# A two-layer graph attention kernel: head 0's denominators and reciprocals moved into its attention product, and its sources' row made by one small product and a VectorE transpose

## The chip, the cores and the metric

The kernel runs on one core of a Trainium2 chip. The metric is the device time of one execution in microseconds. Before the change the median of three runs is 637.04 us (636.98 to 637.24). About 0.2% (1.27 us) is what such a measurement tells from no change.

## The reference

x has 512 nodes of 768 features; the graph has 16896 edges (self loops among them). Two graph attention layers are computed, the first with 8 heads of 768, the second with one, then a residual and a layer norm:

```python
def gat_layer(x, W, a_s, a_d, b, edge_index, concat):
    h = (x @ W).reshape(n, H, C)
    alpha_s = jnp.einsum('nhc,hc->nh', h, a_s)
    alpha_d = jnp.einsum('nhc,hc->nh', h, a_d)
    e = jax.nn.leaky_relu(alpha_s[src] + alpha_d[dst], NEG_SLOPE)
    m = jax.ops.segment_max(e, dst, num_segments=n)
    e = jnp.exp(e - m[dst])
    denom = jax.ops.segment_sum(e, dst, num_segments=n)
    alpha = e / (denom[dst] + EPS)
    msg = h[src] * alpha[:, :, None]
    out = jax.ops.segment_sum(msg, dst, num_segments=n)
    return out + b
...
h = jax.nn.elu(gat_layer(x, W1, ...))
x = _layernorm(x + gat_layer(h, W2, ...))
```

## The kernel before

The edges become a dense 512x512 matrix of counts CT (how often node s is a source of node d), built by products of one-hot blocks on TensorE, 132 blocks of 128 edges. A mask Mk is 0 where there is an edge and very negative elsewhere. With these, each head is dense work in tiles of 128 nodes (NT = 4) and 128 features (FT = 6):

- stage B: h = x W1 of the head, in 8 half products of 18 matmuls (`half_B`); high and low parts of x and W1 give three products each. ScalarE copies each half product from PSUM to h32 (`evict_B`). VectorE takes two sums over each row of h (`sums_h`): asd, the source and the target term of each node.
- the row of sources: the 512 source terms must lie along the free dimension, the same on all partitions, in the PSUM bank "as" of the head. `sources` makes it. For heads 0, 1 and 7 TensorE transposes a broadcast column, four times (`broadcast`, L1303). For heads 2 to 6 VectorE spreads the column over 16 columns (`source_columns`, L803), TensorE sums it with a 128x128 pattern in one product of 16 moving columns (L1311), and VectorE turns the result with a 128x512 transpose (`source_row`, L810).
- scores: VectorE's `maxima` reads that row and the mask (L837, four operations), `terms` makes small columns from the maxima (L844, L846 and three more), `columns` and `rows` turn them into rows, and `scores` on ScalarE and VectorE gives L = exp(...) times CT, and Ph and Pl, its high and low parts.
- denominators: for head 0, y2, the sum of L over the source tiles, goes through four products with two columns of ones (`denominators`, L1339; each fp32 product is two passes, so the profile shows eight). VectorE adds EPS and takes the reciprocal of a 128x4 tile dcl (L907, L909), TensorE turns it into rows by four transposes (`reciprocals`, L1347), and ScalarE copies them to rb (L495). Other heads have another way to rb.
- stage A: the attention product, one per 128 features: 12 matmuls of 512 columns (`stage_A`, L1357, L1360, L1363). VectorE scales it by rb (`scale_A`, L916), then `elu` (L922, L924) and `low_g` (L928), with ScalarE's exp (L510) and high part (L517) between.
- stage C: the head's share of layer 2, added up in the six O banks.

Each engine's program is written out by hand, in the order in which it runs, with semaphore waits between engines. An engine that waits holds up all that stands behind it in its own program. The PSUM banks are O0 to O5 and R0, R1. Uses of R alternate in the order of a list RING, and `take` waits until the use two places back was read. Uses listed in OWN have a fixed O bank and no such wait.

Around the change TensorE's program is: edge blocks, head 1's half products 4 to 7 (with the transposes of CT's mask ahead of number 6, L1432, and then head 0's sources; in the last one also `columns(0)`, L1322), head 2's half products 0 to 3, denominators of head 0, stage A of head 0 for c = 0 to 5 (reciprocals after the second tile of c = 0; sources of head 1 ahead of c = 1), head 2's half products 4 to 7, then stage C of head 0. The last four take the R banks in turn: number 6 waits until ScalarE has copied number 4, number 7 until it has copied number 5. ScalarE's program has these two copies (L455) within its work on head 0's activation:

```python
if h == 0:
    reciprocals()
    e.wait_ge(s_asd, 18)
    high_w2(0, 0)
    high_w2(0, 1)
for c in range(FT):
    exp_y(h, c)
    if c:
        high_g(h, c - 1)
    if h == 0 and c < 2:
        high_w2(0, c + 2)
    if h == 0 and c == 4:
        evict_B(2, 2, 0)
high_g(h, FT - 1)
if h == 0:
    evict_B(2, 2, 1)
```

`high_w2` (L443) gives the high part of a tile of W2; GpSimd's `low_w2` (L1195) waits for it and gives the low part. VectorE's program after head 0's scores is: two low parts of P (L894), L907 and L909, row sums of head 2's first tile (L768), `maxima` (L818, L837) and `terms` of head 1, two more row sums, then `scale_A` and the rest for c = 0 to 5.

Of the kernel before, what the change touches and what calls it, by code (L numbers as in the profile page):

```python
# [5 lines left out]
def gat_resnorm_kernel(nc, x, xT, src, dst, W1, as1, ad1, b1c, W2, as2, ad2, b2, out):  # L6
# [64 lines left out]
    with ctx:  # L71
# [97 lines left out]
        def abc_slot(h):  # L169
# [6 lines left out]
        R = [ctx.enter_context(nc.psum_tensor(f"R{i}", [128, 512], f32)) for i in range(2)]  # L176


        OWN = {("B", 0, 2): O[4], ("B", 0, 3): O[5], ("as", 0, 0): O[4], ("as", 1, 0): O[5], ("den", 0, 0): O[4],
               ("x", 0, 0): O[0], ("r1", 0, 0): O[1], ("x", 1, 0): O[2], ("r1", 1, 0): O[3],  # L180
               ("A", 0, 0): O[2], ("A", 0, 1): O[3], ("A", 0, 2): O[0], ("A", 0, 3): O[1], ("A", 0, 4): O[4], ("A", 0, 5): O[5]}

# [71 lines left out]
        def released(use):  # L254

            kind, h, n = use
            if kind == "B":
                return s_h32, 8 * h + n + 1
            if kind == "al":
                return s_ar, 1  # L260
            if kind == "at":
                return s_asd, 8 * H + 1
            if kind == "as":
                return s_amx, NT * h + NT
            if kind == "xs":
                return s_srow, h - 1
            if kind == "x":
                return s_row, 2 * h + 2
            if kind == "r1":
                return s_lk, NT * (h + n) + NT  # L270
            if kind == "den":
                return (s_dc, h) if 0 < h < EARLY else (s_rc, h + 1)
            if kind == "A":
                return s_y, FT * h + n + 1
            return s_dn0, h + 1
# [443 lines left out]
        def vector_program(e):  # L719
# [79 lines left out]

            def source_columns(h):  # L800

                e.wait_ge(s_asd, 8 * h + 8)
                e.tensor_tensor(asm[:, :, :], by_quarter(asd[:, h % 2, 0, :]), by_tile, ALU.mult).then_inc(s_asm, 1)  # L803

            def source_row(h):
                cols = ring_bank("xs", h, 0)[:, 0:NT * 4]
                e.wait_ge(s_bc, bc_value(h, 0))

                e.wait_ge(*released(RING[RING_AT["as", h, 0] - 2]))
                e.transpose(ring_bank("as", h, 0)[:, :].rearrange("p (c j) -> p c j", j=32), cols.unsqueeze(2).broadcast_to([128, NT * 4, 32])).then_inc(s_srow, 1)  # L810

            def maxima(h, lo, hi, bank):


                if h == 0:
                    e.wait_ge(s_four, 11)
                e.wait_ge(s_asd, 8 * h + 8 if h < H else 8 * H + 1)
                e.tensor_tensor(adm[:, :, :], by_quarter(asd[:, h % 2, 1, :]), by_tile, ALU.mult).then_inc(s_adm, 1)  # L818
                if 2 <= h < H - 1:
                    source_row(h)  # L820
                for t in range(lo, hi):
                    if t == 0:
                        if 2 <= h < H - 1:
                            e.wait_ge(s_srow, h - 1)
                        else:
                            e.wait_ge(s_bc, bc_value(h, 0))
                        if h >= EARLY:
                            e.wait_ge(s_A, FT * h)
                    if h == 0:
                        e.wait_ge(s_mk, t + 1)  # L830
                    if 0 < h < EARLY:

                        if t:
                            e.wait_ge(s_amx, NT * h + t)
                        else:
                            e.wait_ge(s_asd, (18, 24)[h - 1])
                    e.tensor_tensor_reduce(  # L837
                        out=junk[:, 0:N] if 0 < h < EARLY else Pl[:, t, :], in0=bank[:, :], in1=Mk[:, t, :], op0=ALU.add, op1=ALU.max, scale=1.0, scalar=-3e38,
                        accum_out=amx[:, t:t + 1]).then_inc(s_amx, 1)
# [120 lines left out]
            for j in range(EJ):  # L960
                if FIRST <= j < FIRST + FT:
                    low_x(j - FIRST)
                    low_w1(0, j - FIRST)
                if j in (24, 30, 46, 70):
                    t = (24, 30, 46, 70).index(j)
                    if t == 0:
                        wait_abc(0)
                        e.wait_ge(s_xl, FT)
                    e.wait_ge(s_h32, 2 * t + 2)
                    sums_h(0, t, h32[:, t % 2, :], abc[:, 0, :, :])  # L970
                    low_h(0, t)
                if j in range(36, 36 + 6 * FT, 6):
                    low_w1(1, (j - 36) // 6)
                if j in range(78, 78 + 6 * 4, 6):
                    low_w1(2, (j - 78) // 6)
                if j in (44, 76, 98, 124):
                    accumulate((44, 76, 98, 124).index(j))
                one_hot(j)
            wait_abc(1)
            e.wait_ge(s_h32, 10)  # L980
            sums_h(1, 0, h32[:, 0, :], abc[:, 1, :, :])
# [280 lines left out]
        def tensor_program(e):  # L1262
# [42 lines left out]

            def sources(h, ready):

                if 2 <= h < H - 1:
                    bank = take("xs", h, 0)
                    e.wait_ge(s_asm, h - 1)  # L1310
                    e.matmul(bank[:, 0:NT * 4], four[:, :], asm[:, :, :].rearrange("p t b -> p (t b)"), start=True, stop=True).then_inc(s_bc, 1)  # L1311
                    return
                bank = take("as", h, 0)
                e.wait_ge(s_asd, ready)
                broadcast(bank, asd[:, h % 2, 0, :], range(NT))
# [24 lines left out]
                                 start=d == 0, stop=True, skip_group_check=True)  # L1340
                m.then_inc(s_den, 1)

            def reciprocals():

                e.wait_ge(s_rc, 1)
                for d in range(NT):
                    m = e.transpose(ring_bank("den", 0, 0)[:, 128 * d:128 * d + 128], dcl[:, d:d + 1].broadcast_to([128, 128]), idn[:, :])  # L1347
                m.then_inc(s_rt, 1)

            def stage_A(h, c):  # L1350
                bank = take("A", h, c)
                for t in range(NT):
# [8 lines left out]
                    if c == 0:  # L1361
                        e.wait_ge(s_hl, NT * h + t + 1)
                    m = e.matmul(bank[:, :], hl[:, t, cs], Ph[:, t, :], start=False, stop=t == NT - 1)  # L1363
                    if h == 0 and c == 0 and t == 1:
                        reciprocals()
                m.then_inc(s_A, 1)

            def stage_C(h, c, groups=range(6), between=None, ends=True, at=2):
# [54 lines left out]
                count_block(j)  # L1423

            for n in range(4, 8):
                if n == 6:
                    e.wait_ge(s_cst, 4)
                    e.wait_ge(s_ji, 2 * len(GROUPS))
                    e.wait_ge(s_ms, NT)
                    for d in range(NT):  # L1430
                        for s in range(NT):
                            m = e.matmul(O[d][:, 128 * s:128 * s + 128], ohd[:, s, 128 * d:128 * d + 128], idb[:, :],  # L1432
                                         start=s == 0, stop=True, skip_group_check=True)
                        m.then_inc(s_mt, 1)
                    sources(0, 8)
                half_B(1, n // 2, n % 2, take("B", 1, n),
                       (lambda: columns(0, ring_bank("x", 0, 0))) if n == 7 else None)
            for n in range(4):
                half_B(2, n // 2, n % 2, take("B", 2, n))
            denominators(0)  # L1440
            for c in range(FT):
                if c == 1:
                    sources(1, 16)
# [156 lines left out]
```

## Time and profile before

| what | value |
|---|---|
| median of 3 runs | 637.04 us |
| the profiled execution | 636.94 us, span 635.0 us |
| TensorE matmuls busy | 626.7 us (99%) |
| TensorE weight loads busy | 536.9 us (85%) |
| VectorE busy | 536.8 us (85%) |
| ScalarE busy | 337.6 us (53%) |
| GpSimd busy | 210.6 us (33%) |
| mean granted TensorE clock | 0.998 |
| chain that ended last | TensorE 85%, VectorE 10% |

Times in the profile count from the span's start. PE is TensorE's matmuls, PEld its weight loads, DVE VectorE, ACT ScalarE, POOL GpSimd. In a timeline the columns are start, time taken, engine, line, operation, output and inputs, count, and in brackets the idle time before it and who ended it. Starts are given as issued; an operation that is held up inside its engine shows as a long one. Successive matmuls overlap, so a matmul's own time is longer than the distance to the next. In the chain of waits the pieces stand end to end, and each piece's time is what it adds.

### The profile page before, as it was taken

What the parts mean: (1) busy time and instruction counts of PE and PEld (TensorE: products, weight loads), DVE (VectorE), ACT (ScalarE), POOL (GpSimd) and SP (SyncE); (2) the same over time, 40 slices, a digit from 0 to 9 for tenths busy, and PEclk for the clock granted to TensorE, in tenths of its full rate; (3) what the DMA queues carried; (4) which work ended last, traced back from release to release, by engine and by line L of the source; (5) the groups of instructions that cost most, each with busy time, mean ns of one, the idle gap of its engine ahead of it and who ended that gap; (6) DMA issues with size and microseconds to landing.
All of it is one profiled execution on the core that took longest, in us unless ns stands there. A gap on an engine that the chain in (4) does not pass through costs nothing.

```text
span 635.0 us, 9251 instructions
## 1 busy us (share of the span) xinstructions
PE 626.7 (99%) x3353; PEld 536.9 (85%) x3362; DVE 536.8 (85%) x974; ACT 337.6 (53%) x570; POOL 210.6 (33%) x133
## 2 busy tenths in 40 slices
PE   9999999999999999999999999999999999999996
PEld 5766568989888898989899988999898989887885
DVE  8999997989989887778686958797798869898967
ACT  7899992545625645553354635363445344534282
POOL 2000000131643834076405840384208540451230
PEclk9999999999999999999999999999999999999999
DMA  8422403116153423043302520260217130500002
GB/s 321 161 71 81 148 27 100 50 51 199 34 166 122 153 98 102 1 141 109 100 0 71 179 65 11 76 224 19 81 40 233 52 100 6 218 26 0 1 2 99
DMA packets 22172, 59.34 MB, mean 93 GB/s; under 512 B 2544, under 2 KB 2800, under 8 KB 22128
## 3 DMA queue, kind: packets, MB, share of 16 engines
q1 hardware_dynamic: 21984, 58.69, 28.0%
q8 instruction: 27, 0.44, 0.3%
q14 instruction: 17, 0.14, 0.1%
q10 hardware_dynamic: 144, 0.07, 0.0%
HBM read 54.03 MB, written 4.72 MB: 93 GB/s over the span
## 4 chain that ended last, share of the span: by engine, by line
PE 85%; DVE 10%; issue 1%; ACT 1%; DMA 1%; POOL 1%; ACTq 0%; DVEq 0%
PE O L1390 27%; PE R L1281 8%; PE R L1287 8%; PE R L1284 8%; PE O L1298 7%; PE R L1357 6%; PE R L1363 6%; PE R L1360 6%; DVE ohd L728 1%; DVE L L885 1%; PE O L1357 1%; PE O L1363 1%; PE O L1360 1%; PE O L1539 1%; PE O L1545 1%
## 5 line engine op out<-in xcount | busy, mean ns | idle before, releaser
L1195 POOL TENSOR_TENSOR W2l<-Wr,W2h 128x768 fp32r<-128x768 f32 x48 | 91.9, 1935 | 133.3 <-ACT W2h L443 133.3
L1281 PE MATMUL R<-W1h,xTh 128*128 128x384 f32 x312 | 106.1, 340 | 0.4 <-ACT h L455 0.4
L1199 POOL TENSOR_TENSOR Pl<-L,Ph 128x512 fp32r<-128x512 f32 x34 | 55.9, 1662 | 152.4 <-ACT Ph L491 152.4
L1287 PE MATMUL R<-W1h,xTl 128*128 128x384 f32 x312 | 104.8, 336 | 0.0
L1284 PE MATMUL R<-W1l,xTh 128*128 128x384 f32 x312 | 104.8, 336 | 0.0
L1189 POOL TENSOR_TENSOR W1l<-Wr,W1h 128x768 fp32r<-128x768 f32 x30 | 59.6, 2010 | 116.9 <-ACT W1h L432 116.8
L768 DVE CUSTOM_DVE_ANT_0 junk<-h,abc 128x768 bf16<-128x768 f32 x64 | 66.9, 1046 | 23.2 <-ACT h L455 21.6
L1390 PE MATMUL O<-W2h,gh 128*128 128x256 f32 (+1 forms) x384 | 78.2, 338 | 0.0
L1390 PE MATMUL O<-W2h,gl 128*128 128x256 f32 (+1 forms) x384 | 77.8, 337 | 0.0
L1390 PE MATMUL O<-W2l,gh 128*128 128x256 f32 (+1 forms) x384 | 77.2, 335 | 0.0
L1357 PE MATMUL R<-Ph,hh 128*128 128x512 f32 x168 | 66.3, 395 | 0.0
L1363 PE MATMUL R<-Ph,hl 128*128 128x512 f32 x168 | 65.9, 392 | 0.0
L1390 PEld LDWEIGHTS O<-W2l,gh 128*128 128x128 f32 x384 | 59.0, 188 | 7.9
L1360 PE MATMUL R<-Pl,hh 128*128 128x512 f32 x168 | 65.3, 389 | 0.0
L1390 PEld LDWEIGHTS O<-W2h,gl 128*128 128x128 f32 x384 | 58.7, 188 | 7.7
L1390 PEld LDWEIGHTS O<-W2h,gh 128*128 128x128 f32 x384 | 58.3, 188 | 6.5 <-issue 0.2
L1281 PEld LDWEIGHTS R<-W1h,xTh 128*128 128x128 f32 x312 | 58.5, 188 | 2.4 <-ACT h L455 1.2
L443 ACT CAST W2h<-Wr 128x768 fp32r<-128x768 f32 x48 | 37.9, 832 | 42.0 <-DVE rm L853 19.2
L1298 PE MATMUL O<-ohd,ohs 128*128 128x512 bf16 x255 | 59.1, 379 | 1.1 <-DVE ohs L732 0.4
L455 ACT COPY h<-R 128x384 f32<-128x384 f32 x62 | 29.4, 475 | 57.1 <-PE R L1287 54.6
L1284 PEld LDWEIGHTS R<-W1l,xTh 128*128 128x128 f32 x312 | 58.5, 188 | 0.6
L1287 PEld LDWEIGHTS R<-W1h,xTl 128*128 128x128 f32 x312 | 58.5, 188 | 0.0
(201 smaller groups left out, 1178.3 us busy)
## 6 DMA issues: line engine op xcount, KB each, us to landing
Wr<-in_W SPq DMA_DIRECT2D x101, 384.0 KB, 3.6
abc<-in_as SPq DMA_DIRECT2D x9, 384.0 KB, 4.1
abc<-in_ad SPq DMA_DIRECT2D x9, 384.0 KB, 5.3
h_rows<-h SPq DMA_DIRECT2D x8, 384.0 KB, 2.3
hl<-h_rows SPq DMA_DIRECT2D x8, 384.0 KB, 5.9
xin<-in_xT SPq DMA_DIRECT2D x6, 256.0 KB, 5.7
xr<-in_x SPq DMA_DIRECT2D x1, 1536.0 KB, 7.7
out<-res SPq DMA_DIRECT2D x4, 384.0 KB, 2.3
```

Of the source, the lines that this page charges most:

```text
L768: e.tensor_tensor_reduce(out=junk[:, :], in0=get, in1=a_ap[:, i, :], op0=ALU.mult, op1=ALU.add, scale=1.0, scalar=0.0, accum_out=asd[:, h ...
L1189: e.tensor_tensor(W1l[:, k, :], Wr[:, n, :], W1h[:, k, :].bitcast(f32), ALU.subtract).then_inc(s_w1l, 1)
L1195: e.tensor_tensor(W2l[:, m % N2, :], Wr[:, n, :], W2h[:, m % N2, :].bitcast(f32), ALU.subtract).then_inc(s_w2l, 1)
L1199: e.tensor_tensor(Pl[:, t, d0:d1], L[:, t, d0:d1], Ph[:, t, d0:d1].bitcast(f32), ALU.subtract).then_inc(s_Pl, 1)
L1281: e.matmul(bank[:, 0:HALF], xTh[:, f, xs], hi[:, ws], start=f == 0, stop=False)
L1284: e.matmul(bank[:, 0:HALF], xTh[:, f, xs], lo[:, ws], start=False, stop=False)
L1287: m = e.matmul(bank[:, 0:HALF], xTl[:, f, xs], hi[:, ws], start=False, stop=f == FT - 1)
L1298: e.matmul(O[2 * (g % 2) + q][:, :], ohs[:, r, 128 * q:128 * q + 128], ohd[:, r, :], start=j == STARTS[g], stop=j == STARTS[g + 1] - 1).th ...
L1357: e.matmul(bank[:, :], hh[:, t, cs], Ph[:, t, :], start=t == 0, stop=False)
L1360: e.matmul(bank[:, :], hh[:, t, cs], Pl[:, t, :], start=False, stop=False)
L1363: m = e.matmul(bank[:, :], hl[:, t, cs], Ph[:, t, :], start=False, stop=t == NT - 1)
L1390: mm = e.matmul(ob, ga[:, c, 128 * t:128 * t + 128], wa[:, q, lo:hi], start=first and (hi - lo == 512 or t % 2 == 0), stop=last, skip_grou ...
```

## The change

Two things are done, both for head 0 alone.

Head 0's row of sources is made in the way of heads 2 to 6: `source_columns(0)` stands on VectorE behind the last edge block, one product of 16 columns into O5 ahead of head 1's half product 5, and VectorE's transpose from O5 to O4 after the first step of `maxima(0)`.

`denominators(0)` no longer stands ahead of stage A but in its first product (c = 0), after the second tile, where the reciprocals were; the reciprocals go to the same place in the second product (c = 1).

```diff
-        OWN = {("B", 0, 2): O[4], ...
+        OWN = {("xs", 0, 0): O[5], ("B", 0, 2): O[4], ...
...
             if kind == "xs":
-                return s_srow, h - 1
+                return s_srow, h
...
             def source_columns(h):
+                if h == 0:
+                    e.wait_ge(s_four, 11)
...
             def source_row(h):
                 cols = ring_bank("xs", h, 0)[:, 0:NT * 4]
                 e.wait_ge(s_bc, bc_value(h, 0))
-                e.wait_ge(*released(RING[RING_AT["as", h, 0] - 2]))
+                if h:
+                    e.wait_ge(*released(RING[RING_AT["as", h, 0] - 2]))
...
-                if 2 <= h < H - 1:
+                if h != 1 and h < H - 1:
                     source_row(h)
                 for t in range(lo, hi):
                     if t == 0:
-                        if 2 <= h < H - 1:
-                            e.wait_ge(s_srow, h - 1)
+                        if h != 1 and h < H - 1:
+                            e.wait_ge(s_srow, max(h, 1))
...
                 one_hot(j)
+            source_columns(0)
             wait_abc(1)
...
             def sources(h, ready):
-                if 2 <= h < H - 1:
+                if h != 1 and h < H - 1:
                     bank = take("xs", h, 0)
-                    e.wait_ge(s_asm, h - 1)
+                    e.wait_ge(s_asm, max(h, 1))
...
-            def reciprocals():
+            def reciprocals_0(h):
...
-                    if h == 0 and c == 0 and t == 1:
-                        reciprocals()
+                    if h == 0 and c < 2 and t == 1:
+                        (denominators, reciprocals_0)[c](0)
...
             for n in range(4, 8):
+                if n == 5:
+                    e.wait_ge(s_four, 6)
+                    sources(0, 8)
                 if n == 6:
...
-                    sources(0, 8)
...
-            denominators(0)
             for c in range(FT):
```

The order of instructions moves as follows; the changed kernel's line numbers are 3 to 7 higher than the old ones behind the first edit. On TensorE, from the last matmul of head 2's half product 3 into stage A of head 0 (oner holds ones, dcl the reciprocals, idn the identity), before:

```order
L1287 MATMUL R<-W1h,xTl 128x384
L1339 MATMUL O<-oner,y 128x2 x4
L1357 MATMUL O<-Ph,hh 128x512
L1360 MATMUL O<-Pl,hh 128x512
L1363 MATMUL O<-Ph,hl 128x512
L1357 MATMUL O<-Ph,hh 128x512
L1360 MATMUL O<-Pl,hh 128x512
L1363 MATMUL O<-Ph,hl 128x512
L1347 MATMUL O<-idn,dcl 128x128 x4
L1357 MATMUL O<-Ph,hh 128x512
```

and after the change, from the third matmul of the first product's first tile:

```order
L1367 MATMUL O<-Ph,hl 128x512
L1361 MATMUL O<-Ph,hh 128x512
L1364 MATMUL O<-Pl,hh 128x512
L1367 MATMUL O<-Ph,hl 128x512
L1343 MATMUL O<-oner,y 128x2 x4
L1361 MATMUL O<-Ph,hh 128x512
L1364 MATMUL O<-Pl,hh 128x512
L1367 MATMUL O<-Ph,hl 128x512
L1361 MATMUL O<-Ph,hh 128x512
L1364 MATMUL O<-Pl,hh 128x512
L1367 MATMUL O<-Ph,hl 128x512
L1307 MATMUL O<-idn,asd 128x128 x4
```

The denominators stand six attention matmuls later than before. The reciprocals no longer stand in this product; head 1's source transposes (L1307) come ahead of them, and then six matmuls of the second product, behind which they stand.

On VectorE, at the start of head 0's maxima, before:

```order
L768 ISA asd 128x1
L818 TENSOR_TENSOR adm<-asd,quad 128x16
L837 ISA Pl,amx<-O4,Mk 128x512
L837 ISA amx 128x1
L837 ISA Pl,amx<-O4,Mk 128x512
```

and after:

```order
L768 ISA asd 128x1
L821 TENSOR_TENSOR adm<-asd,quad 128x16
L813 STREAM_TRANSPOSE O4<-O5 128x512
L840 ISA Pl,amx<-O4,Mk 128x512
L840 ISA amx 128x1
```

The transpose is new there. All else on VectorE, but for the small multiply behind the last edge block, keeps its order, and so do ScalarE, GpSimd and SP.

## Rows read from the trace of the kernel before

**Rows 1.** Waits of TensorE's weight loads, 145:635: who, for whom, us, times, longest.
```profile
PEld R L1281 <- ACT h L455: 1.2, 3, 0.7
```
**Rows 2.** Timeline of ScalarE's copies of h, then of TensorE's weight load.
```profile
151.58 0.47 ACT L455 COPY h<-R 128x384 f32<-128x384 f32 x1
...
155.21 0.47 ACT L455 COPY h<-R 128x384 f32<-128x384 f32 x1
...
155.73 0.19 PEld L1281 LDWEIGHTS R<-W1h,xTh 128*128 128x128 f32 x1 [0.24 <-ACT h L455]
```
**Rows 3.** Chain that ended last, 107:114: start, us added, engine, tile, line, count.
```profile
108.06 0.44 PE O L1303 x4
...
113.05 0.17 PE R L1287
113.22 0.14 PE O L1322 x2
113.36 0.26 PE R L1281
```
**Rows 4.** The same chain at head 0's denominators, and at the tail's (L1553).
```profile
127.64 1.02 PE O L1339 x8
128.67 0.34 PE O L1357
129.01 0.23 PE O L1360
...
619.33 0.79 PE R L1553 x8
```
**Rows 5.** Timeline of TensorE: head 2's fourth half product's end, and the reciprocals.
```profile
127.16 0.34 PE L1287 MATMUL R<-W1h,xTl 128*128 128x384 f32 x1
...
130.00 0.60 PE L1347 MATMUL O<-idn,dcl 128*128 128x128 f32 x4
```
**Rows 6.** The line of heads 2 to 6's transpose: ns min/median/max.
```profile
L810 DVE STREAM_TRANSPOSE R<-R x5: 721/731/732, 180.6 to 475.2; 128x512 f32<-128x512 f32 x5
```
**Rows 7.** Timeline of VectorE, 108:139.
```profile
108.53 0.69 DVE L837 CUSTOM_DVE_ANT_0 Pl<-O,Mk 128x512 fp32r<-128x512 f32 x1 [1.30 <-PE O L1303]
...
115.57 0.96 DVE L768 CUSTOM_DVE_ANT_0 junk<-h,abc 128x768 bf16<-128x768 f32 x1 [0.47 <-ACT h L455]
...
128.71 0.16 DVE L907 TENSOR_SCALAR dcl<-O 128x4 f32<-128x4 f32 x1
...
131.00 0.17 DVE L818 TENSOR_TENSOR adm<-asd,quad 128x16 f32<-128x16 f32 x1
132.47 0.69 DVE L837 CUSTOM_DVE_ANT_0 junk<-O,Mk 128x512 bf16<-128x512 f32 x1 [1.30 <-PE O L1303]
...
135.40 0.30 DVE L844 TENSOR_TENSOR zm<-amx,asd 128x4 f32<-128x4 f32 x1
135.74 0.18 DVE L846 TENSOR_TENSOR zmm<-zm,quad 128x16 f32<-128x16 f32 x1
...
138.22 1.28 DVE L916 TENSOR_TENSOR L<-O,rb 128x512 f32<-128x512 f32 x2
```
**Rows 8.** Timeline of ScalarE's copy to rb, and of GpSimd's first pair.
```profile
130.64 0.59 ACT L495 COPY rb<-O 128x512 f32<-128x512 f32 x1 [2.62 <-PE O L1347]
...
132.03 3.65 POOL L1195 TENSOR_TENSOR W2l<-Wr,W2h 128x768 fp32r<-128x768 f32 x2 [5.81 <-ACT W2h L443]
```
**Rows 9.** Timeline at head 6's terms: GpSimd, then VectorE.
```profile
475.14 3.67 POOL L1189 TENSOR_TENSOR W1l<-Wr,W1h 128x768 fp32r<-128x768 f32 x2 [27.30 <-ACT W1h L432]
478.77 1.84 POOL L1195 TENSOR_TENSOR W2l<-Wr,W2h 128x768 fp32r<-128x768 f32 x1
...
478.50 0.33 DVE L844 TENSOR_TENSOR zm<-amx,asd 128x4 f32<-128x4 f32 x1
478.86 1.78 DVE L846 TENSOR_TENSOR zmm<-zm,quad 128x16 f32<-128x16 f32 x1
```
**Rows 10.** Stretch behind the last matmul: us, each engine's busy us, PEclk, DMA share, GB/s.
```profile
629.70:632.60 2.90, 0.00 (x0) 0.00 (x0) 2.09 (x6) 0.98 (x2) 0.00 (x0) 0.96 0.64 257
```

More of the change, by code:

```diff
@@ L176, in gat_resnorm_kernel @@
         R = [ctx.enter_context(nc.psum_tensor(f"R{i}", [128, 512], f32)) for i in range(2)]
-        OWN = {("B", 0, 2): O[4], ("B", 0, 3): O[5], ("as", 0, 0): O[4], ("as", 1, 0): O[5], ("den", 0, 0): O[4],
+        OWN = {("xs", 0, 0): O[5], ("B", 0, 2): O[4], ("B", 0, 3): O[5], ("as", 0, 0): O[4], ("as", 1, 0): O[5], ("den", 0, 0): O[4],
                ("x", 0, 0): O[0], ("r1", 0, 0): O[1], ("x", 1, 0): O[2], ("r1", 1, 0): O[3],
```

## The prediction

> **What bounds the kernel now.** I read the waits of TensorE's weight loads first, then TensorE's chain around the moved operations, then the timelines of VectorE, ScalarE and GpSimd from 107 to 156 us. Behind the edge counts TensorE sets the end, and waits only for fractions of a microsecond: for ScalarE's evictions of h it is 1.2 us in three places [rows 1], and one of the three, 0.24 us at 155.73, lies right behind this change [rows 2]. That place decides the forecast. Head 2's seventh and eighth half products share the two R banks with the fifth and sixth. ScalarE empties those only between its steps of head 0's activation (151.58 and 155.21, [rows 2]), and these follow VectorE's scale, ELU and low parts one for one. So between VectorE's first scaled tile of head 0 and the eviction at 155.21 **VectorE's chain and TensorE are level**, TensorE even 0.24 us early. Work saved on TensorE ahead of that place is worth nothing unless VectorE comes earlier too, and a delay of VectorE there is paid in full by the end.
>
> **TensorE, part by part.**
> 1. Head 0's sources. The four transposes take 0.44 us of the chain [rows 3]. The new product (16 moving columns) is nearest to the one with 32: 0.14 us, and 0.26 instead of 0.17 for the matmul behind it, 0.23 together [rows 3]. Gain 0.44 - 0.23 = 0.2 us (0.1 to 0.3, if the sides differ). It is issued one half product (18 matmuls of 0.17, 3.1 us) ahead of its old place, and its input comes from a VectorE step put right behind the last edge block, so nobody waits for it.
> 2. Head 0's denominators. They start only at 127.64, when VectorE's sum of the exponentials is there, while head 2's fourth half product ended at 127.16 + 0.34 = 127.50; the first attention matmul ends at 128.67 + 0.34 = 129.01 [rows 4, 5]. Without them it would end at 127.50 + 0.23 = 127.73, so they cost 1.28 us. Inside a running product the price is that of the same eight passes in the tail: 0.79 us, and 0.34 instead of 0.23 behind them, 0.90 together [rows 4]. Gain 0.38 us (between 0.1, if TensorE then meets VectorE's low part of block 1, and 0.5).
> 3. The reciprocals' four transposes are only moved: same count, same price.
>
> So TensorE would run 0.2 + 0.38 = 0.6 us earlier from 129 us on. That is all the change saves directly.
>
> **VectorE up to 127 us.** It gains a 16-column multiply and a 128x512 transpose, 0.73 us in five places now [rows 6], and loses the 1.30 us that it waits for TensorE's transposes before head 0's maxima [rows 7]. Later it waits 0.47 us for h at 115.57 anyway [rows 7], which levels the rest; from there it follows TensorE, 0.2 us earlier. I cost this part at nothing more; it would start to cost if the transpose ran over 1.0 us longer (0.57 + 0.47).
>
> **VectorE from 127 us.** The denominators now come behind six attention matmuls. The product starts at 127.16 + 0.17 - 0.2 = 127.1, six matmuls of 0.23 [rows 4] bring it to 128.5, and the passes take 1.02 us to their end [rows 4]: 129.5. VectorE's small step that stood at 128.71 is 0.8 us late. What lies behind it ran to 131.00 [rows 7], so VectorE is ready for head 1's maxima at 131.0 + 0.8 + 0.1 = 131.9. Now these start at 132.47, after 1.30 us of waiting for head 1's source transposes [rows 7]. Those start at 128.5 + 0.9 + 6 x 0.23 = 130.8 after the change and end 0.6 later, at 131.4: no longer in the way. Head 1's maxima, and its first term (135.40 now), come 0.6 us **earlier**: 134.8. Taken alone a gain.
>
> **What the move costs: GpSimd.** The reciprocals' transposes (130.00, [rows 5]) go behind head 1's source transposes and six matmuls of the second product: 130.8 + 0.44 + 6 x 0.23 = 132.6, that is 2.6 us later. ScalarE's copy to rb moves with them, from 130.64 to 133.25 [rows 8]. Behind that copy on ScalarE stand the first two high parts of W2, and GpSimd's low parts hang on them: two operations, 3.65 us, from 132.03 now [rows 8], from 134.65 to 138.3 then. Now they run beside head 1's maxima (132.47 to 135.4), which read one tensor in PSUM and one in SBUF and keep their 0.69 us [rows 7]. Then they will run beside head 1's terms and two row sums, which read two SBUF tensors each.
>
> What that does, the trace shows at head 6: GpSimd's pair ends at 478.81, its next operation at 480.61; VectorE's first term, issued at 478.50, takes 0.33 us and ends at 478.83; the second, issued at 478.86, takes 1.78 us and ends at 480.64 [rows 9]. A small two-tensor operation of VectorE is held until GpSimd's running one ends, and where GpSimd has another ready, that gets in and holds VectorE's next. Today's own row shows it in small: the term at 135.40 takes 0.30 us, to 135.70, and GpSimd's pair ends at 135.68 [rows 7, 8]. The Trainium skill ("Advanced Engine Details and Errata", GPSIMD Details) says that GpSimd shares a read and a write interface with VectorE and conflicts with its instructions that have two SBUF inputs. By that rule, which speaks against the change as these rows do, the sum has the same sign.
>
> Transferred: first term issued at 134.8, held by GpSimd's first operation (134.65 to 136.45); the second held by GpSimd's second, to 138.3. Now the second term ends at 135.74 + 0.18 = 135.92 [rows 7]. **VectorE is late by 138.3 - 135.9 = 2.4 us**, its first scaled tile comes at 140.6 instead of 138.22. From there to the eviction ScalarE's steps and GpSimd's next pair follow VectorE, and all of it moves as a whole: the evictions come at 154.0 and 157.6. TensorE, 0.6 us early, reaches head 2's seventh half product near 151.9, waits 2.5 us, waits 0.5 us more before the eighth, and starts that at 155.73 + 2.4 = 158.1.
>
> **Sum.** TensorE's 0.6 us end in that wait. What reaches the end is +2.4 us; what follows depends on TensorE and VectorE, both late by the same, so nothing takes it back. SP's two loads of W2 that wait for GpSimd's pair move by 2.6 us, tens of microseconds ahead of their use: nothing. The profiled execution took 636.94 us (span 635.0), 0.1 under the median of 637.04; so 639.3 for such a one, **639.4** for the median. Bounds: +1.9, if GpSimd's pair starts 0.5 us sooner than I have it, to +2.9, if it starts that much later: 638.9 to 640.0.
>
> **The rivals.**
> - *No hold (not slower).* VectorE's terms stay short. Then VectorE and TensorE are both 0.6 us early, and so is the end: 636.4. For it: GpSimd is only some 0.2 us ahead of the first term. Against: if it came behind, it would hold the second, and the sums behind are of the same kind. It decides if the pair starts over 2 us earlier, under the maxima as now.
> - *One hand-over.* GpSimd's first operation holds the term to 136.45, VectorE then keeps the way for the rest of the terms and the sums (2.8 us now, 135.40 to 138.22), and GpSimd's second waits. First scaled tile at 139.2, end +0.9: 637.9. Against: the second hand-over in [rows 9].
> - *TensorE's clock.* A TensorE gap of 2.5 us is new. Behind the last matmul of the kernel the granted clock over 629.70 to 632.60 is 0.96 [rows 10]: it fell to half (1.2 of 2.4 GHz) in the last 0.23 us of that stretch, after 2.7 us of idling. If it falls in the gap, the seventh half product takes 6.2 instead of 3.1 us and ends 1.2 us behind the eviction at 158.1: 640.6. The Trainium skill ("TensorE: Matmul & The Clock Gate", What's actually happening) says that the lower clock is the default and activity releases it; by it this case can occur, and the price is the same.
> - *Faster.* That would take 1.27 us and more; the whole saving is 0.6.
>
> **Chances and range.** My forecast 0.70; the clock's fall 0.07; one hand-over 0.06; no hold 0.14; faster by more 0.03. A measurement of this kernel can tell about 0.2% (1.27 us) from no change: faster 0.03, same 0.06 + 0.14 = 0.20, slower 0.77. The range takes in the forecast with its bounds, the one hand-over (637.9) and the clock (640.6): 637.8 to 640.8.
>
> **What would show it.** After: the denominators' passes at 0.9 us within the first product; ScalarE's copy to rb near 133.3; GpSimd's first pair near 134.7; head 1's first two terms at about 1.6 and 1.8 us; the first scaled tile near 140.6; TensorE's weight loads waiting for ScalarE's h before head 2's seventh and eighth half products, 3 us together. Wrong: terms of 0.15 us, GpSimd's pair under the maxima, or no TensorE wait between 150 and 160 us.

## The result, and the profile after

| | before | after |
|---|---|---|
| median of six executions | 637.13 us | 639.52 us |
| lowest to highest | 636.98 to 637.24 | 639.00 to 639.98 |
| profiled execution, its span | 636.94, 635.0 | 639.1, 637.3 |
| time after / before | | 1.0037 [1.0026, 1.0047] |

The change makes the kernel 2.4 us, 0.37%, slower. The six executions fall in two groups, 639.0 to 639.3 and 639.7 to 640.0 us; the one profiled is of the lower group. What parts the groups was found last (below).

The page of the changed kernel, its engine totals and the start of its chain by engine:

```profile
span 637.3 us, 9251 instructions
PE 627.4 (98%) x3351; PEld 537.1 (84%) x3360; DVE 540.7 (85%) x976; ACT 337.4 (53%) x570; POOL 210.6 (33%) x133
...
PE 75%; DVE 20%; issue 2%; ACT 1%; POOL 1%; DMA 1%; DVEq 0%; ACTq 0%
```

VectorE is busy 3.9 us longer than before and TensorE 0.7; the totals do not say where the end became 2.3 us later. The waits of TensorE's weight loads from 100 us on do (engine, line, what for: us in total, times, longest):

```profile
PEld R L1285 <- ACT h L455: 4.0, 4, 2.8
...
PEld O L1364 <- DVE Pl L897: 0.2, 1, 0.2
```

The first line stood at 1.2 us in three waits before [rows 1]; the second, a wait for VectorE's low part of P in the first attention product, is new and short. The timeline of the weight loads of the changed kernel around head 2's seventh and eighth half products:

```profile
151.87 0.19 PEld L1291 LDWEIGHTS R<-W1h,xTl 128*128 128x128 f32 x1
154.84 0.19 PEld L1285 LDWEIGHTS R<-W1h,xTh 128*128 128x128 f32 x1 [2.78 <-ACT h L455]
...
158.47 0.19 PEld L1285 LDWEIGHTS R<-W1h,xTh 128*128 128x128 f32 x1 [0.51 <-ACT h L455]
```

TensorE stands still for 2.78 us and then 0.51 us, and the eighth half product starts at 158.47 instead of 155.73 [rows 2]. To see why the evictions of h come late, follow VectorE and GpSimd 20 us earlier. VectorE of the changed kernel, from the denominators' small step to the first scaled tile:

```profile
129.79 0.16 DVE L910 TENSOR_SCALAR dcl<-O 128x4 f32<-128x4 f32 x1 [1.02 <-PE O L1343]
...
132.31 0.69 DVE L840 CUSTOM_DVE_ANT_0 junk<-O,Mk 128x512 bf16<-128x512 f32 x1
...
135.25 1.57 DVE L847 TENSOR_TENSOR zm<-amx,asd 128x4 f32<-128x4 f32 x1
136.85 1.79 DVE L849 TENSOR_TENSOR zmm<-zm,quad 128x16 f32<-128x16 f32 x1
138.68 0.18 DVE L851 SCALAR_TENSOR_TENSOR mcm<-zmm 128x16 f32<-128x16 f32 x1
...
140.95 1.28 DVE L919 TENSOR_TENSOR L<-O,rb 128x512 f32<-128x512 f32 x2
```

ScalarE's copy to rb, and GpSimd's low parts of W2, in the same kernel:

```profile
133.56 0.59 ACT L495 COPY rb<-O 128x512 f32<-128x512 f32 x1 [5.48 <-PE O L1351]
...
134.95 3.66 POOL L1199 TENSOR_TENSOR W2l<-Wr,W2h 128x768 fp32r<-128x768 f32 x2 [8.66 <-ACT W2h L443]
```

GpSimd's two operations run from 134.95 to 138.61, each about 1.84 us. VectorE's term on 128x4 numbers is issued 0.3 us behind the first one and ends at 136.82, when that one ends; the next term ends at 138.64, when the second one ends. Before they took 0.30 and 0.18 us [rows 7]. The two terms are 2.9 us longer together, for no work of their own. Head 1's maxima begin a little earlier than before (132.31 against 132.47), and the first scaled tile comes at 140.95 instead of 138.22 [rows 7].

The chain of the changed kernel at two pieces of TensorE, the sources' product and the moved denominators:

```profile
104.25 0.13 PE O L1315 x2
104.38 0.27 PE R L1285
...
128.97 0.80 PE O L1343 x8
```

The sources' product adds 0.13 us to the chain, and the matmul behind it 0.27 instead of 0.17, against 0.44 for the transposes [rows 3]. The denominators' eight passes add 0.80.

### The profile page after: what moved, and what is told of

It is laid out like the page before. It is cut to its first block, busy times and chain, and to the rows that moved or that the text cites. A ratio compares the mean times of both kernels' runs of the same rounds, so it can differ in the third digit from the quotient of the medians.

```text
span 637.3 us, 9251 instructions
## 1 busy us (share of the span) xinstructions
PE 627.4 (98%) x3351; PEld 537.1 (84%) x3360; DVE 540.7 (85%) x976; ACT 337.4 (53%) x570; POOL 210.6 (33%) x133
## 4 chain that ended last, share of the span: by engine, by line
PE 75%; DVE 20%; issue 2%; ACT 1%; POOL 1%; DMA 1%; DVEq 0%; ACTq 0%
PE O L1394 27%; PE R L1285 8%; PE R L1291 7%; PE R L1288 7%; PE R L1361 6%; PE R L1367 6%; PE R L1364 6%; DVE ohd L728 4%; PE O L1302 3%; DVE ohs L732 2%; DVE junk L768 2%; DVE W1l L754 1%; DVE L L888 1%; DVE gl L931 1%; PE O L1544 1%
```

## The experiments

Each was timed beside the kernel before on the same chip; its median there was 637.16 us with the first group (1 to 4), 637.19 with the second (5 to 8), 637.33 with the third (9 and 10), 637.16 with the last (11 and 12). The brackets behind a ratio are its 95% interval. Gains of 0.8 to 1 us, as in experiments 1, 4 and 9, are smaller than the 1.27 us named at the start, and their intervals leave out 1 only just; they are read together with the profiles.

### 1 and 2. Each half of the change alone

Experiment 1 keeps the kernel before and takes the sources' part:

```diff
 def source_columns(h):
+    if h == 0:
+        e.wait_ge(s_four, 11)
...
+            source_columns(0)
             wait_abc(1)
...
 def sources(h, ready):
-    if 2 <= h < H - 1:
+    if h != 1 and h < H - 1:
```

> The new way to head 0's row of sources alone; denominators and reciprocals stand where they stood before the change. Theory of the hold (the loss comes from GpSimd's first pair of low parts of W2 falling on head 1's terms): the reciprocals keep their place, so the pair still runs under head 1's maxima, the terms stay below 0.35 us, and TensorE and VectorE both come 0.1 to 0.2 us earlier: 0.1 to 0.2 us under the kernel before. Rival, that VectorE's new transpose (0.72 us) is paid: 0.3 to 0.7 us over the kernel before.

Measured: 636.35 us, ratio 0.9986 [0.9978, 0.9995]: 0.8 us **faster**, where 0.1 to 0.2 was expected. The hold (a VectorE operation that ends only when GpSimd's ends) is absent: GpSimd's pair stands at 131.82, the terms take 0.30 and 0.18 us, and TensorE waits 0.26 us at 155.55, as before. The sources' new way is not what costs. But it brings 0.6 us too much; experiment 9 looks for that.

Experiment 2 takes the other half, the denominators and the reciprocals:

```diff
-                    if h == 0 and c == 0 and t == 1:
-                        reciprocals()
+                    if h == 0 and c < 2 and t == 1:
+                        (denominators, reciprocals_0)[c](0)
...
-            denominators(0)
             for c in range(FT):
```

> Denominators and reciprocals moved into the attention products, head 0's sources as before. Theory of the hold: the whole loss is here, 2.3 to 2.7 us over the kernel before, with head 1's first two terms at 1.5 and 1.8 us. Rival, that the loss is TensorE's own (the denominators' passes cost more inside a product): the stage would be longer on TensorE with terms below 0.35 us, and the loss could not exceed some 1 us.

Measured: 640.85 us, ratio 1.0057 [1.0041, 1.0072]: 3.7 us slower, a microsecond more than the most that was expected. The held terms are there, in VectorE's timeline of experiment 2:

```profile
135.31 1.57 DVE L844 TENSOR_TENSOR zm<-amx,asd 128x4 f32<-128x4 f32 x1
136.91 1.78 DVE L846 TENSOR_TENSOR zmm<-zm,quad 128x16 f32<-128x16 f32 x1
```

and so is the wait of 2.77 us at 154.88. The rest lies behind it. The first of the next stretches, in us: busy time of PE, PEld, DVE, ACT and POOL with counts, granted clock of TensorE, DMA share, GB/s:

```profile
153.00:156.00 3.00, 1.11 (x6) 1.11 (x7) 2.85 (x6) 1.62 (x3) 0.00 (x0) 0.97 0.71 279
156.00:159.00 3.00, 3.00 (x11) 3.00 (x10) 2.88 (x6) 2.16 (x5) 0.00 (x0) 0.50 0.02 9
```

Over 156 to 159 us the granted clock is 0.50, 1.2 of 2.4 GHz, behind the gap of 2.8 us. In TensorE's timeline of experiment 2 the matmuls of the half product first follow each other by 0.17 us, then by 0.32:

```profile
155.17 0.34 PE L1284 MATMUL R<-W1l,xTh 128*128 128x384 f32 x1
155.34 0.34 PE L1287 MATMUL R<-W1h,xTl 128*128 128x384 f32 x1
...
157.16 0.53 PE L1281 MATMUL R<-W1h,xTh 128*128 128x384 f32 x1
157.48 0.53 PE L1284 MATMUL R<-W1l,xTh 128*128 128x384 f32 x1
```

No wait for the eighth half product is left; it comes later than the eviction by itself. So the clock's rival, given 0.07 in the prediction, happens here, and the profile of the changed kernel shown above does not have it.

### 3. The late pair alone, nothing else of the change

The kernel before, with ScalarE's first two high parts of W2 held back until head 1's second maximum is taken; of the instructions only those two and GpSimd's pair behind them are put off:

```diff
                     reciprocals()
 
-                    e.wait_ge(s_asd, 18)
+                    e.wait_ge(s_amx, NT + 2)
                     high_w2(0, 0)
                     high_w2(0, 1)
```

> The kernel before, with nothing moved; only ScalarE starts the first two high parts of W2 later (when two of head 1's four maxima are there instead of when head 2's first row sums are), so that GpSimd's pair starts near 134.9 us. Theory of the hold: GpSimd's first operation holds head 1's first term, its second the second, the first scaled tile comes 2.5 us late and the end is 2.3 to 2.8 us over the kernel before, though TensorE's program is untouched. Rival, that the late denominators are the cause: no change (within 0.2 us), since W2's parts are needed only 20 us later.

Measured: 640.63 us, ratio 1.0054 [1.0040, 1.0068], +3.5 us. VectorE's, then GpSimd's timeline of experiment 3:

```profile
135.43 1.32 DVE L844 TENSOR_TENSOR zm<-amx,asd 128x4 f32<-128x4 f32 x1
136.78 1.78 DVE L846 TENSOR_TENSOR zmm<-zm,quad 128x16 f32<-128x16 f32 x1
...
140.87 1.28 DVE L916 TENSOR_TENSOR L<-O,rb 128x512 f32<-128x512 f32 x2
```

```profile
134.88 3.65 POOL L1195 TENSOR_TENSOR W2l<-Wr,W2h 128x768 fp32r<-128x768 f32 x2 [8.61 <-ACT W2h L443]
```

The mechanism stands without any instruction of the change. TensorE waits 2.37 us at 154.74, and here too its clock falls (0.61 over 156 to 159 us): the first scaled tile is 2.65 us late, and about 1 us more is then the clock's, so +3.5 came out and not the expected 2.3 to 2.8.

### 4. The change without the late pair

The changed kernel, with ScalarE making the two high parts before it waits for the reciprocals (and after the first of head 2's two row sums, not the second):

```diff
-                    reciprocals()
 
-                    e.wait_ge(s_asd, 18)
+                    e.wait_ge(s_asd, 17)
                     high_w2(0, 0)
                     high_w2(0, 1)
+                    reciprocals()
```

> The changed kernel, with ScalarE's first two high parts of W2 ahead of its copy to rb, started when the first of head 2's first two row sums is there, so that GpSimd's pair starts near 132.1 us and runs under head 1's maxima. Theory of the hold: terms at 0.3 to 0.5 and 0.2 us, first scaled tile 2.5 us earlier than in the changed kernel, and the end 0.2 to 0.4 us under the kernel before (VectorE sets it, TensorE has 0.3 us to spare). Rival, late denominators are the cause: the end stays 2 us and more over the kernel before.

Measured: 636.21 us, ratio 0.9986 [0.9977, 0.9995], 0.9 us faster than before and 3.3 faster than the change as made. VectorE's, then GpSimd's timeline of experiment 4:

```profile
135.01 0.55 DVE L847 TENSOR_TENSOR zm<-amx,asd 128x4 f32<-128x4 f32 x1
135.59 0.17 DVE L849 TENSOR_TENSOR zmm<-zm,quad 128x16 f32<-128x16 f32 x1
```

```profile
131.87 3.67 POOL L1199 TENSOR_TENSOR W2l<-Wr,W2h 128x768 fp32r<-128x768 f32 x2 [5.82 <-ACT W2h L443]
```

The pair ends at 135.54, so it catches only the first term, which ends at 135.56. Another order of ScalarE's statements undoes all of the loss.

### 10. One operation late instead of two

A dose between none and both, on the kernel before:

```diff
                     high_w2(0, 0)
+                    e.wait_ge(s_amx, NT + 2)
                     high_w2(0, 1)
```

> Half a dose: the kernel before, with only the second of ScalarE's two high parts held back until two of head 1's maxima are there. GpSimd's first operation runs under the maxima, the second starts near 134.9 us. Theory of the hold: one hand-over, the first term is held to 136.7, the second is short; VectorE 1.0 us late, and the end 0.8 to 1.2 us over the kernel before, with a TensorE gap too short for the clock to fall. Rival, that the lateness of ScalarE or of W2's parts counts and not the hold: the same 2.4 us and more as with both late, or none.

Measured: 638.30 us, ratio 1.0016 [1.0007, 1.0025], +1.0 us. VectorE's, then GpSimd's timeline of experiment 10:

```profile
135.62 1.32 DVE L845 TENSOR_TENSOR zm<-amx,asd 128x4 f32<-128x4 f32 x1
136.97 0.17 DVE L847 TENSOR_TENSOR zmm<-zm,quad 128x16 f32<-128x16 f32 x1
```

```profile
132.25 1.84 POOL L1196 TENSOR_TENSOR W2l<-Wr,W2h 128x768 fp32r<-128x768 f32 x1 [5.81 <-ACT W2h L443]
135.07 1.85 POOL L1196 TENSOR_TENSOR W2l<-Wr,W2h 128x768 fp32r<-128x768 f32 x1 [0.98 <-ACT W2h L443]
```

One operation of GpSimd holds one term (ends 136.92 and 136.94), and the second term is free again. TensorE's waits are 0.79 and 0.56 us, its clock stays at 1.00 from 153 to 159 us. One term is held for each operation of GpSimd that is ready: on this step the forecast chose between +0.9 and +2.4, and it goes by the number of GpSimd's operations.

### 5 to 8. The level place at 155 us

The prediction said that VectorE's chain and TensorE are level before ScalarE's eviction at 155.21 [rows 2], so that TensorE's saving is worth nothing and VectorE's delay counts in full. These four move head 2's two evictions forward on ScalarE, ahead of steps of the activation, in four kernels: 5, the change; 6, the change with the early pair; 7, before; 8, the sources' half.

```diff
+                    if h == 0 and c == FT - 1:
+                        evict_B(2, 2, 1)
                     if c:
                         high_g(h, c - 1)
...
-                    if h == 0 and c == 4:
+                    if h == 0 and c == 3:
                         evict_B(2, 2, 0)
...
                 high_g(h, FT - 1)
-                if h == 0:
-                    evict_B(2, 2, 1)
```

> The changed kernel, with ScalarE's copies of head 2's fifth and sixth half products each one step earlier among its steps of head 0's activation (the sixth ahead of the last but one high part, where ScalarE is idle). VectorE stays 2.4 us late. If TensorE's wait runs through these two copies, its gap before the seventh half product goes from 2.8 us to under 0.5, and what is left of VectorE's lateness meets TensorE later, at head 0's share of layer 2 (it needs head 1's scores): 0.5 to 1.8 us over the kernel before, and the clock does not fall there. Rival, that VectorE's lateness is paid somewhere else: the same 2.4 us and more over the kernel before.

> The changed kernel with both remedies: GpSimd's pair started under head 1's maxima, and the two copies one step earlier. With the tie gone TensorE keeps its 0.6 us: 0.6 to 1.4 us under the kernel before, 0.2 to 0.5 under the version with the early pair alone. Rival, that VectorE takes over elsewhere: no difference to the version with the early pair alone.

> The kernel before with the two copies one step earlier and nothing else: TensorE loses its wait of 0.24 us at 155.7, 0.1 to 0.3 us under the kernel before. Rival: no change.

> Head 0's sources in the new way, denominators as before, and the two copies one step earlier. Set against the version with both remedies it tells what the move of the denominators is worth once nothing takes its gain: that one should be 0.3 to 0.5 us faster than this one, which should come 0.2 to 0.3 us under the version with the new sources alone. Rival, that the move is worth nothing at all: both the same.

| | evictions as they were | evictions earlier |
|---|---|---|
| before | 637.1 to 637.3 (medians) | 637.05, 0.9997 [0.9988, 1.0006] (7) |
| the change | 639.52 | 638.14, 1.0014 [1.0005, 1.0024] (5) |
| the change, early pair | 636.21 (4) | 635.66, 0.9975 [0.9966, 0.9985] (6) |
| sources alone | 636.35 (1) | 636.15, 0.9985 [0.9976, 0.9994] (8) |

(Experiment 7 has one execution at 1621.9 us, far from all others; without it the median is 637.04.)

- The move of the denominators and reciprocals is worth 0.14 us with the evictions in their old place (4 against 1) and 0.5 us with them earlier (6 against 8). The second is near the 0.38 that the prediction gave TensorE as its saving. Between medians whose own spread is some tenths the first is nothing and the second just beyond that. The traces say the same. From head 0's product with 16 columns to head 2's, behind the level place, are 75.75 us in 4 (103.85 to 179.60) against 75.88 in 1 (103.76 to 179.64), 0.13 less; and 75.19 in 6 (103.82 to 179.01) against 75.57 in 8 (104.14 to 179.71), 0.38 less, which is the forecast's figure. The saving is real and ended in the wait.
- The late pair costs 2.5 us even there (5 against 6). TensorE then meets VectorE's delay elsewhere. The weight loads of experiment 5 (neither of the last two waits is in the profiles of before and of experiment 6):

```profile
152.07 0.19 PEld L1285 LDWEIGHTS R<-W1h,xTh 128*128 128x128 f32 x1 [0.28 <-ACT h L455]
...
166.19 0.19 PEld L1394 LDWEIGHTS O<-W2h,gh 128*128 128x128 f32 x1 [1.98 <-DVE L L882]
186.34 0.19 PEld L1361 LDWEIGHTS R<-Ph,hh 128*128 128x128 f32 x1 [0.49 <-DVE amx L840]
```

The delay belongs to VectorE's chain, and the eviction was only the first place where TensorE met it.
- Experiment 7 expected a gain of 0.1 to 0.3 us; its interval (0.8 faster to 0.4 slower) holds that and no change: inconclusive. In its profile the wait at 155.7 is gone and head 2's 16-column product comes at 179.59 instead of 179.78, but TensorE waits 1.38 us at head 6 where before waited 1.20 (see experiment 9).
- Experiment 6 beats both kernels: 1.5 us under before, 3.9 under the change.

### 9. Two instructions more on VectorE, for nothing

Experiments 1, 4, 6 and 8 were all some tenths of a microsecond faster than the places studied so far explain. Their waits at head 6 differ from those of the kernel before. There VectorE of before has a gap between two small steps:

```profile
480.68 0.17 DVE L848 SCALAR_TENSOR_TENSOR mcm<-zmm 128x16 f32<-128x16 f32 x1
481.11 0.17 DVE L852 TENSOR_TENSOR rm<-adm,mcm 128x16 f32<-128x16 f32 x1 [0.26 <-DVE mcm L848]
```

and TensorE's weight loads of before wait 1.20 us in what follows:

```profile
494.93 0.19 PEld L1281 LDWEIGHTS R<-W1h,xTh 128*128 128x128 f32 x1 [0.24 <-DVE L L879]
498.69 0.19 PEld L1281 LDWEIGHTS R<-W1h,xTh 128*128 128x128 f32 x1 [0.67 <-ACT h L455]
502.08 0.19 PEld L1281 LDWEIGHTS R<-W1h,xTh 128*128 128x128 f32 x1 [0.29 <-ACT h L455]
```

The changed kernel waits 0.73 us there (two waits), and has no gap. It, and all kernels with the sources' half, have two more VectorE instructions ahead. So the kernel before gets two whose results nobody reads:

```diff
                 one_hot(j)
+            e.wait_ge(s_four, 11)
+            e.wait_ge(s_asd, 8)
+            e.tensor_tensor(asm[:, :, :], by_quarter(asd[:, 0, 0, :]), by_tile, ALU.mult)
+            e.tensor_tensor(mcm[:, :, :], by_quarter(asd[:, 0, 0, :]), by_tile, ALU.mult)
             wait_abc(1)
```

> The kernel before with two small multiplies more on VectorE (128x16, into tiles that are written again before anyone reads them) behind the last edge block, where VectorE waits 3 us for the last counts. Nothing else is changed. The new way to head 0's sources also puts two more instructions on VectorE ahead of the heads, and in all kernels with it a gap of 0.26 us between two of VectorE's terms of head 6 is gone and TensorE's waits there are 0.5 us shorter. Theory: this gap belongs to the place in VectorE's program, so it is gone here too, and the end comes 0.3 to 0.6 us earlier than the kernel before. Rival, the gap has to do with the sources themselves or with their timing: the gap stays, no change in time.

Measured: 636.53 us, ratio 0.9988 [0.9979, 0.9997]: 0.8 us **faster** by doing more. VectorE's, then TensorE's weight loads' timeline of experiment 9:

```profile
480.72 0.17 DVE L848 SCALAR_TENSOR_TENSOR mcm<-zmm 128x16 f32<-128x16 f32 x1
480.93 0.17 DVE L852 TENSOR_TENSOR rm<-adm,mcm 128x16 f32<-128x16 f32 x1
```

```profile
498.27 0.19 PEld L1285 LDWEIGHTS R<-W1h,xTh 128*128 128x128 f32 x1 [0.42 <-ACT h L455]
501.67 0.19 PEld L1285 LDWEIGHTS R<-W1h,xTh 128*128 128x128 f32 x1 [0.28 <-ACT h L455]
```

The gap is gone and the waits fall to 0.70 us, 0.5 less. The wait at 155.78, 0.26 us, is as before. All other profiles agree: the gap stands in the five kernels without the two instructions (before, 2, 3, 7, 10), with waits of 1.20 to 1.47 us there, and in none of the nine profiles with them, where the waits are 0.64 to 0.89 us. So most of what experiment 1 won need not be the sources' product: two instructions more on VectorE win as much. The waits account for 0.5 of the 0.8 us, and the two profiled spans differ by 0.4 (634.6 and 635.0); the rest lies inside the interval (0.2 to 1.3 us). That the gap and the longer waits come and go with these two instructions is shown. What makes the gap, whether the number of instructions ahead is what counts, and whether the gap alone makes the waits, was not found.

### 11 and 12. The changed kernel again, for the clock

The same kernel, unaltered, in seven more executions, two of them profiled, to learn what parts its two groups.

> The changed kernel again, unaltered, to catch the clock. In its first six executions three took 639.0 to 639.3 us and three 639.7 to 640.0. Theory: in the longer ones TensorE's granted clock falls behind the 2.8 us wait before head 2's seventh half product, for part of it, as it did with the denominators moved alone. Then executions spread over 639.0 to 640.4 us, and one profiled above 639.6 shows a mean granted clock below 0.9 between 155 and 159 us, matmuls spaced over 0.2 us there, a shorter wait or none for the eighth half product, and head 2's 16-column product at 182.8 to 183.7 us; one profiled below 639.4 shows the clock at 1.00 there and that product near 182.5. Rival: the longer ones come from elsewhere (a load, another wait); then the clock is 1.00 over 155 to 159 us and that product stands near 182.5 in a long one too.

> The same kernel, one more profiled execution, for the same question: a span above 637.8 us goes with a clock below 1.00 between 155 and 159 us and the 16-column product later than 182.8 us, a span below 637.5 us with the clock at 1.00 and the product near 182.5 us. The rival expects no such tie.

Measured: 639.51 us (638.94 to 640.37), ratio 1.0037 [1.0025, 1.0049], and 639.95. Both profiled executions (640.06 and 639.95 us) are of the upper group. The stretches of experiment 11, then of 12:

```profile
153.00:156.00 3.00, 1.24 (x7) 1.24 (x8) 2.88 (x5) 1.62 (x3) 0.00 (x0) 1.00 0.66 262
156.00:159.00 3.00, 3.00 (x12) 3.00 (x11) 2.88 (x6) 2.28 (x5) 0.00 (x0) 0.55 0.00 0
159.00:162.00 3.00, 3.00 (x17) 3.00 (x17) 2.33 (x5) 2.79 (x6) 0.00 (x0) 0.88 0.33 131
```

```profile
153.00:156.00 3.00, 1.44 (x4) 1.45 (x5) 2.88 (x6) 1.62 (x3) 0.00 (x0) 0.69 0.61 238
156.00:159.00 3.00, 3.00 (x14) 3.00 (x14) 2.88 (x5) 2.49 (x6) 0.00 (x0) 0.74 0.03 10
159.00:162.00 3.00, 3.00 (x18) 3.00 (x18) 2.33 (x5) 2.80 (x5) 0.00 (x0) 1.00 0.31 124
```

The execution profiled first, of the lower group, has 1.00 in the same stretch:

```profile
156.00:159.00 3.00, 2.82 (x16) 2.49 (x16) 2.88 (x6) 2.20 (x5) 0.00 (x0) 1.00 0.03 10
```

All three have the same wait of 2.78 us. In the lower group the half product runs at full clock and TensorE waits 0.51 us for the eighth. In the upper the clock is down before the product starts (12: its first matmuls are 0.32 us apart) or falls some 1.6 us into it (11), and there is no second wait. From head 0's 16-column product to head 2's are 78.40 us in the first (104.09 to 182.49), 79.48 in experiment 11 (104.02 to 183.50) and 79.34 in 12 (103.82 to 183.16): the fall costs 1.1 and 0.9 us. The rival, another cause for the upper group, falls in these two. Of 13 executions of the changed kernel 7 lie above 639.7 us, and the mean granted clock over the whole span, known for each, parts them too: 0.998 in the six of the lower group, 0.995 to 0.997 in the seven of the upper. It is 0.995 to 0.997 in all eight executions of experiments 2 and 3 as well. By itself this mean is a weak sign: of 67 executions of the kernel before, five have 0.997.

## Why the prediction was right, and where it was not

It gave 639.4 us, 637.8 to 640.8, and slower at 0.77; measured are 639.52 and +0.37%. The changed kernel's profile starts this part 0.3 us late (the multiply before head 0's maxima at 107.33 instead of 107.06), which is taken off in the last column. It is not of the change: in experiment 12, the same kernel, this multiply stands at 107.06.

| step | predicted | in the profile, less 0.3 |
|---|---|---|
| denominators' passes in the first product | 0.9 us | 0.80 (128.97 in the chain), 0.09 on the next matmul (followed after 0.32 us, not 0.23) |
| head 1's first term | 134.8 | 134.95 |
| copy to rb | 133.25 | 133.3 |
| GpSimd's pair | 134.65 | 134.65 |
| the two terms | 1.6 and 1.8 us | 1.57 and 1.79 |
| first scaled tile | 140.6 | 140.65 |
| waits for h | 2.5 and 0.5 us | 2.78 and 0.51 |
| eighth half product | 158.1 | 158.2 |

**What bounds the kernel: right.** Experiments 5 to 8 show both halves, TensorE's saving worth about nothing with the evictions in place and some 0.5 us without the tie.

**The cost of the moved reciprocals: right, in place, size and cause.** Experiment 3 makes it without the change, 4 takes it away from the change, 10 has one held term instead of two and +1.0 us. The rule of the Trainium skill ("Advanced Engine Details and Errata", GPSIMD Details) that GpSimd conflicts with VectorE's instructions with two SBUF inputs agrees: the maxima, with one input in PSUM, take 0.69 us with GpSimd's pair beside them in experiment 4, as without. The rival "one hand-over" fell by the second term's 1.79 us; "no hold" fell with it.

**The sources' product: right in place, 0.2 us** (0.44 less 0.13 and 0.10 on the next matmul). Head 0's maxima no longer wait for TensorE, but start only at 108.75, after 0.61 us of waiting for ScalarE's Mk; the prediction had no such wait. It had costed this part at nothing, and that holds, since VectorE still waits 0.31 us for h at 115.63.

**"Nothing takes it back": wrong by 0.4 us.** In the profile of the lower group head 2's 16-column product is 2.7 us late (182.49 against 179.78), 2.4 less the late start, and the end 2.3, or 2.0. The step that failed is the assumption that behind 158 us all stays as it is. With the two new VectorE instructions the gap at head 6 is gone, as in experiment 9, and TensorE's waits there fall from 1.20 to 0.73 us. No step of the working looked at what adding instructions does to instructions far behind them.

**The clock: its chance far too small, and its price near the measured one by a slip.** The prediction gave the fall 1.2 us and 0.07. It costs 0.9 to 1.1 us and occurs in about half of the executions. The 1.2 does not follow from its own terms: a half product of 6.2 us, begun when the wait ends at 154.4, would end at 160.6, 2.5 us behind 158.1, and give 641.9 us, outside the range. The term that was wrong is the 6.2 us, half the clock for the whole half product. In experiment 11 it takes 4.65 us (154.76 to 159.41), because the clock is back before its end (0.88 over 159 to 162 us); in experiment 12 it takes 4.62 us. The prediction also named the clock's fall after 2.7 us of idling [rows 10] and forecast a wait of 2.5 us: that row should have made it an open case. That the lower clock is the default and activity releases it (the Trainium skill, "TensorE: Matmul & The Clock Gate", What's actually happening) fits the rows in which it comes back during steady matmuls: 0.55, then 0.88 in experiment 11, 0.74, then 1.00 in 12.

The gain at head 6 and the clock, both left out of the sum, go against each other. Without both the time would be near 639.5 (an estimate, 639.1 and 0.4); with the gain at head 6 alone it is 639.1, the lower group, and the clock lifts half of the executions to 639.7 and more, so that the median falls between the groups. That 639.4 met 639.5 so closely is in part luck; that the change loses 2 us and more, and by which waits, is not.

## What to carry to other kernels

A step that is moved off the critical engine takes along everything queued behind its consumer: here TensorE saved 0.4 us and ScalarE's copy, moved 2.6 us later, carried a GpSimd operation onto the wrong VectorE instructions. Follow the queue of each engine that reads the moved result until nothing is left that starts at another time, and ask what runs beside it now; where an order on that engine can be changed (the early pair, experiment 4), the loss goes. Before shortening an engine that is level with another, move the point where they meet (experiment 6), or its saving ends in the wait. And let a TensorE wait like these, of 2.4 to 2.8 us, count for more than its length.

## What the runs showed of the hardware that was not expected

- In these traces a small VectorE operation with two SBUF inputs, issued while a GpSimd operation runs, ends only when that one ends (the 128x16 term takes 0.17 us free and up to 1.79 held), and a second operation that GpSimd has ready holds VectorE's next one: VectorE does not keep the way once it has it. Known from [rows 9], it was confirmed in number by experiments 3, 4 and 10.
- Behind the same TensorE gap of 2.78 us the clock falls in some executions and not in others (two of three profiles of the changed kernel), and it falls before the work behind the gap (12) or some 1.6 us into it (11). Behind a gap of 0.79 us (experiment 10) and of 1.98 us (experiment 5) no fall was seen in the profiled execution.
- A VectorE gap of 0.26 us between two small instructions comes and goes with two unrelated instructions 385 us ahead of it, and with it some 0.5 us of TensorE waits. A comparison of two versions within some tenths of a microsecond can be decided by this alone; of the 0.8 us that experiment 1 won, all may be of this kind, since experiment 9 wins as much with no part of the change.
